# Ranking edges in a gather pass: running sums on VectorE and four TensorE products in place of sixteen

## The reference, cut to what matters

```
def _rel_graph_conv(x, W, W_loop, b, src, dst, etypes, num_nodes):
    xw = jnp.einsum('nd,rdh->rnh', x, W)
    msg = xw[etypes, src]
    agg = jax.ops.segment_sum(msg, dst, num_segments=num_nodes)
    return agg + x @ W_loop + b
h = _rel_graph_conv(features, W1, loop1, b1, src, dst, etypes, n)
h = jax.nn.relu(h)
h = _rel_graph_conv(h, W2, loop2, b2, src, dst, etypes, n)
```

## Time and profile before

| | us |
|---|---|
| median of 3 runs (12566.58 to 12575.17) | 12574.69 |
| span of the profiled execution, which is all that is known of its own time | 15198.0 |
| ranking pass g0, first gather to last, in the profile | 2704.8 |
| plain pass g1, first gather to last, in the profile | 2412.6 |

### The profile page before, as it was taken

The page is one execution under the profiler, slowest core; times in us unless marked ns, Lnnn a source line. Parts: engine busy times, 40 slices in busy tenths (PEclk is TensorE's granted clock), DMA queues, the critical chain, the costliest instruction groups (busy, mean ns, idle before and its releaser), DMA issues. The chain is left out here.

```text
span 15198.0 us, 174858 instructions
## 1 busy us (share of the span) xinstructions
PE 7352.3 (48%) x42682; PEld 5826.6 (38%) x42906; DVE 5571.9 (37%) x10022; ACT 2825.4 (19%) x7817; POOL 8278.1 (54%) x8916
## 2 busy tenths in 40 slices
PE   7444444463323324333333886777777773333332
PEld 4343333332222223333232764555555553222222
DVE  5444444431111113212111886655555654111111
ACT  4000000020000002111111004555555553000000
POOL 1555656626666664666666124444444444666665
PEclk8666666676565666556666997777777776565565
DMA  4111111141111111111111761111111111222222
GB/s 179 40 40 40 40 40 40 42 156 45 45 45 45 45 45 51 43 44 43 43 44 43 187 150 45 38 38 38 38 38 38 39 38 49 47 47 47 47 47 58
DMA packets 628740, 846.66 MB, mean 56 GB/s; under 512 B 167762, under 2 KB 464219, under 8 KB 628212
## 3 DMA queue, kind: packets, MB, share of 16 engines
q0 software_dynamic: 270448, 573.37, 14.6%
q1 hardware_dynamic: 225848, 205.13, 4.3%
q10 hardware_dynamic: 131916, 62.14, 1.6%
HBM read 598.43 MB, written 244.10 MB: 55 GB/s over the span
## 5 line engine op out<-in xcount | busy, mean ns | idle before, releaser
L1206 POOL DMA_INDIRECT GF<-TAB,IDXA x3322 | 3212.3, 967 | 2220.4 <-issue 1197.2
L1250 PE MATMUL PSUM<-GF,OH 128*128 x10560 | 2292.5, 401 | 4035.2 <-SPq L1191 2396.1
L1250 PEld LDWEIGHTS PSUM<-GF,OH 128*128 128x128 f32 x10560 | 2095.4, 302 | 4213.9 <-issue 4213.3
L1774 POOL DMA_INDIRECT GF<-HTAB,IDS x1760 | 1678.9, 954 | 1754.4 <-PE PSUM L1951 1015.8
L1123 DVE TENSOR_TENSOR OH<-PSUM,DLOA 128x1024 f32<-128x1024 f32 x660 | 804.4, 1222 | 4346.5 <-remote 1927.9
L1533 POOL DMA_INDIRECT MSG<-GF,IDS x1661 | 1610.5, 970 | 1072.7 <-ACT GF L1463 584.1
L1206 POOL DMA_INDIRECT GF<-HROW,IDXA x1661 | 1570.9, 946 | 949.3 <-issue 475.6
L1521 PE MATMUL PSUM<-ACC,SCR 128*128 x3520 | 736.5, 388 | 1198.4 <-ACT PSUM L1441 1029.4
L2031 DVE TENSOR_REDUCE SM<-PSUM 128x8 f32<-128x1024 f32 x880 | 1074.7, 1221 | 311.4 <-remote 208.0
L1521 PEld LDWEIGHTS PSUM<-ACC,SCR 128*128 128x128 f32 x3520 | 675.9, 289 | 1234.1 <-issue 1234.0
L1489 DVE CAST SCR<-PSUM 128x1024 f32<-128x1024 bf16 x220 | 269.4, 1225 | 2043.1 <-remote 1551.7
(11 more groups left out here) (388 smaller groups left out, 10841.7 us busy)
## 6 DMA issues: line engine op xcount, KB each, us to landing
GF<-MSG ACTq DMA_DIRECT2D x880, 66.0 KB, 2.2
GF<-MSG SPq DMA_DIRECT2D x880, 66.0 KB, 2.2
GF<-TAB,IDXA POOLq DMA_INDIRECT x3322
TAB<-SCR SPq DMA_DIRECT2D x100, 512.0 KB, 2.6
TAB<-OH SPq DMA_DIRECT2D x96, 512.0 KB, 2.6
GF<-HTAB,IDS POOLq DMA_INDIRECT x1760
MSG<-GF,IDS POOLq DMA_INDIRECT x1661
GF<-HROW,IDXA POOLq DMA_INDIRECT x1661
```

Of the source, the lines that this page charges most:

```text
L1206: q.indirect_dma_start(G[:, t % RING, k, 0:row], None, table, bass.IndirectOffsetOnAxis(ap=IDXA[:, at:at + 1], axis=0)).then_inc(s_got[t % ...
L1250: m = q.matmul(PSUM[:, bass.ds(places[k], w)], OH[:, r % 2, k, :], GW[:, bass.ds(rows[k], w)], start=False, stop=False, skip_group_check=True)
L1774: q.indirect_dma_start(GT[:, r, k, :], None, HTAB, bass.IndirectOffsetOnAxis(ap=IDS[:, r, k:k + 1], axis=0)).then_inc(s_got[r], 16)
```

## The change

DVE builds the one-hots with the key outermost and nine slots for each key, of which slot 0 stays zero (`KO` is 98 x 9). A `tensor_tensor_scan` over all 882 elements, with a constant `CARRY` that is 0 at slot 0 and 1 elsewhere, makes running sums of the slots into `BEFORE`, restarting at each key. Slot k of `BEFORE` then counts the tiles before tile k of the whole octet, and slot 8 counts all eight. PE needs one product with `ONESB` over these sums and one with `USTB` over the one-hots for each half: four products of 392, 392, 490 and 392 columns. The 98 extra columns are the octet's totals; DVE adds them to `SOFAR` once for each octet, and `RK` is read only once, at the start. `counted` with its eight small products, and both copies of `RK` are gone, and so are the six products of L1409. PE's moving operands, and the one-hots that DVE multiplies by, are now read with a step of nine bf16 elements (18 bytes). A new semaphore `s_one` orders the one-hots ahead of the scan; `keys` now waits for the products of the octet before the last one.

```diff
-            KO = SCR[:].rearrange("p a c -> p (a c)").bitcast(BF16)[:, 0:2 * K * NB].rearrange("p (u k b) -> p u k b", u=2, k=K)
+            wide = SCR[:].rearrange("p a c -> p (a c)").bitcast(BF16)
+            KO, BEFORE = (wide[:, i * 2 * (K + 1) * NB:(i + 1) * 2 * (K + 1) * NB].rearrange("p (u b k) -> p u b k", u=2, k=K + 1) for i in range(2))
+            CARRY = ST6[:].rearrange("p b c -> p (b c)").bitcast(BF16)[:, 0:(K + 1) * NB]
...
-            RK, WITHIN = PS[4][:, 0:NB], [PS[5 + h][:, 0:HALF * NB] for h in range(2)]
+            RK, WITHIN = PS[4][:, 0:NB], [PS[5 + h][:, 0:(HALF + h) * NB].rearrange("p (k b) -> p k b", b=NB) for h in range(2)]
...
-                        wait(q, s_rk, 2 * (t - 1) + 1)
-                        q.tensor_tensor(KO[:, r % 2], bcast(IOTP[:, 0:NB].unsqueeze(1), P, K, NB),
-                                        bcast(KEYS[:, bass.ds(t * K, K)].unsqueeze(2), P, K, NB), ALU.is_equal).then_inc(s_key, 1)
+                        wait(q, s_w, 2 * (t - 1))
+                        one = KO[:, r % 2, :, 1:K + 1]
+                        q.tensor_tensor(one, bcast(IOTP[:, 0:NB].unsqueeze(2), P, NB, K),
+                                        bcast(KEYS[:, bass.ds(t * K, K)].unsqueeze(1), P, NB, K), ALU.is_equal).then_inc(s_one, 1)
+                        q.wait_ge(s_one, t + 1)
+                        q.tensor_tensor_scan(BEFORE[:, r % 2].rearrange("p b k -> p (b k)"), CARRY,
+                                             KO[:, r % 2].rearrange("p b k -> p (b k)"), 0.0, ALU.mult, ALU.add).then_inc(s_key, 1)
...
-                        at, own_keys = PLACE[h], KO[:, r % 2, h * HALF:(h + 1) * HALF, :]
-                        q.wait_ge(s_rk, 2 * t + h + 1)
-                        q.tensor_copy(SOFAR[h], RK).then_inc(s_far, 1)
+                        at, own_keys = PLACE[h], KO[:, r % 2, :, 1 + h * HALF:1 + (h + 1) * HALF].rearrange("p b k -> p k b")
                         q.wait_ge(s_w, 2 * t + h + 1)
-                        q.wait_ge(s_far, 2 * t + h + 1)
-                        q.tensor_tensor(at, WITHIN[h].rearrange("p (k b) -> p k b", k=HALF), bcast(SOFAR[h].unsqueeze(1), P, HALF, NB),
-                                        ALU.add).then_inc(s_t, 1)
+                        if h:
+                            q.tensor_tensor(SOFAR[(r + 1) % 2], SOFAR[r % 2], WITHIN[1][:, HALF, :], ALU.add).then_inc(s_far, 1)
+                            q.wait_ge(s_far, t + 2)
+                        q.tensor_tensor(at, WITHIN[h][:, 0:HALF, :], bcast(SOFAR[r % 2].unsqueeze(1), P, HALF, NB), ALU.add).then_inc(s_t, 1)
...
-                        q.matmul(WITHIN[h], USTB[:], KO[:, r % 2, h * HALF:(h + 1) * HALF, :].rearrange("p k b -> p (k b)"), start=True, stop=False,
+                        lo = h * HALF
+                        q.matmul(WITHIN[h], ONESB[:], BEFORE[:, r % 2, :, lo:lo + HALF + h].rearrange("p b k -> p k b"), start=True, stop=False,
                                  skip_group_check=True)
-                        for k in range(HALF - 1):
-                            n = HALF - 1 - k
-                            m = q.matmul(WITHIN[h][:, (k + 1) * NB:].rearrange("p (k b) -> p k b", k=n), ONESB[:],
-                                         bcast(KO[:, r % 2, h * HALF + k, :].unsqueeze(1), P, n, NB), start=False, stop=k == HALF - 2,
-                                         skip_group_check=True)
-                        m.then_inc(s_w, 1)
-
-                    def counted(r, t, h):
...
-                        for k in range(HALF):
-                            m = q.matmul(RK, ONESB[:], KO[:, r % 2, h * HALF + k, :], start=False, stop=False, skip_group_check=True)
-                        m.then_inc(s_rk, 1)
+                        q.matmul(WITHIN[h][:, 0:HALF, :], USTB[:], KO[:, r % 2, :, lo + 1:lo + 1 + HALF].rearrange("p b k -> p k b"), start=False,
+                                 stop=True, skip_group_check=True).then_inc(s_w, 1)
```

More of the change, by code:

```diff
@@ L1302, in ranked_pass @@
                 "oh", "mm", "io", "land", "bias", "fr", "free", "kept", "open"))
-            s_kb, s_key, s_w, s_far, s_t, s_pos, s_rk = (own(tag + n) for n in ("kb", "key", "w", "far", "t", "pos", "rk"))
+            s_kb, s_one, s_key, s_w, s_far, s_t, s_pos, s_rk = (own(tag + n) for n in ("kb", "one", "key", "w", "far", "t", "pos", "rk"))
             s_got = [sem(tag + f"got{r}") for r in range(RING)]
             HALF = K // 2
-            KO = SCR[:].rearrange("p a c -> p (a c)").bitcast(BF16)[:, 0:2 * K * NB].rearrange("p (u k b) -> p u k b", u=2, k=K)
+            wide = SCR[:].rearrange("p a c -> p (a c)").bitcast(BF16)
+            KO, BEFORE = (wide[:, i * 2 * (K + 1) * NB:(i + 1) * 2 * (K + 1) * NB].rearrange("p (u b k) -> p u b k", u=2, k=K + 1) for i in range(2))
+            CARRY = ST6[:].rearrange("p b c -> p (b c)").bitcast(BF16)[:, 0:(K + 1) * NB]
             KEYS = POSA[:, 0:NTG * K]
             PLACE = [WT[:, h * HALF * NB:(h + 1) * HALF * NB].rearrange("p (k b) -> p k b", k=HALF) for h in range(2)]
-            RK, WITHIN = PS[4][:, 0:NB], [PS[5 + h][:, 0:HALF * NB] for h in range(2)]
+            RK, WITHIN = PS[4][:, 0:NB], [PS[5 + h][:, 0:(HALF + h) * NB].rearrange("p (k b) -> p k b", b=NB) for h in range(2)]
             SOFAR = [HT[:, h, 0:NB] for h in range(2)]
@@ L1388, in _ @@
                     q.tensor_copy(KEYS, KEYS.bitcast(I32)).then_inc(s_kb, 1)
-                    q.wait_ge(s_kb, 2)
+                    q.memset(CARRY, 1.0).then_inc(s_kb, 1)
+                    q.wait_ge(s_kb, 3)
+                    q.memset(CARRY.rearrange("p (b k) -> p b k", k=K + 1)[:, :, 0], 0.0).then_inc(s_kb, 1)
+                    q.memset(KO[:, :, :, 0], 0.0).then_inc(s_kb, 1)
+                    q.wait_ge(s_rk, 1)
+                    q.tensor_copy(SOFAR[0], RK).then_inc(s_far, 1)
+                    q.wait_ge(s_kb, 5)
+                    q.wait_ge(s_far, 1)
                     keys(0, 0)
@@ L1404, in within @@
                         wait(q, s_t, 2 * (t - 1) + h + 1)
-                        q.matmul(WITHIN[h], USTB[:], KO[:, r % 2, h * HALF:(h + 1) * HALF, :].rearrange("p k b -> p (k b)"), start=True, stop=False,
+                        lo = h * HALF
+                        q.matmul(WITHIN[h], ONESB[:], BEFORE[:, r % 2, :, lo:lo + HALF + h].rearrange("p b k -> p k b"), start=True, stop=False,
                                  skip_group_check=True)
-                        for k in range(HALF - 1):
-                            n = HALF - 1 - k
-                            m = q.matmul(WITHIN[h][:, (k + 1) * NB:].rearrange("p (k b) -> p k b", k=n), ONESB[:],
-                                         bcast(KO[:, r % 2, h * HALF + k, :].unsqueeze(1), P, n, NB), start=False, stop=k == HALF - 2,
-                                         skip_group_check=True)
-                        m.then_inc(s_w, 1)
-                    def counted(r, t, h):
-                        if not is_tile(t):
-                            return
-                        q.wait_ge(s_far, 2 * t + h + 1)
-                        for k in range(HALF):
-                            m = q.matmul(RK, ONESB[:], KO[:, r % 2, h * HALF + k, :], start=False, stop=False, skip_group_check=True)
-                        m.then_inc(s_rk, 1)
+                        q.matmul(WITHIN[h][:, 0:HALF, :], USTB[:], KO[:, r % 2, :, lo + 1:lo + 1 + HALF].rearrange("p b k -> p k b"), start=False,
+                                 stop=True, skip_group_check=True).then_inc(s_w, 1)
                     def body(j, r, g):
@@ L1426, in body @@
                             within(r, g, h)
-                        for h in range(2):
-                            counted(r, g, h)
                     passes(q, body)
```

## The result

The changed kernel takes 12721.87 us (12716.33 to 12726.31), the kernel before 12572.74: a ratio of 1.0117, 95% interval 1.0105 to 1.0129. It is 149 us slower, where 130 us faster was forecast.

The account below looks back on a forecast made before the run. The PE/DVE chain was taken to bound ranking pass g0 at 9.93 us a step; falling to 8.15, below the gathers' 9.51, it should save 130 us: 12575 - 130 = 12445 us, range 12330 to 12530.

Parts of the forecast that it names:

- the PE/DVE chain: Ranking pass g0: PE and DVE set the pace at 9.93 us a step, falling to 8.15.
- The bound of the gathers: Whole kernel: 8404 gathers at 1.26 us plus stages between passes make 12247 us, leaving 328 of the median for waits.
- 292: Ranking pass g0 against plain pass g1: ranking costs 292 us in the profile, the most cheaper ranking could give back.
- The effect on the gathers: POOL in g0: the scan costs the gathers nothing, since POOL's times stay 0.95 us beside L1371 with two SBUF operands.
- If the scan slows the gathers' 1.26: Sign of being wrong, in g0: the scan lengthens the 1.26 us from one gather to the next.
- The scan's price: DVE in g0: the 882-element scan takes 1.6 us, with 1.07 and 5.9 as ends.
- the prediction's foot of 0.17 us: DVE sums: fixed time of 0.17 us beside a slope of 1.02 ns an element.
- The strided reads: PE in g0: four products with an 18-byte step take 1.40 us, as fast as packed columns.
- The slower rival: PE in g0: strided products over 3.5 us make the kernel slower, 12725 us at 3 times packed; chance 0.10.
- DVE and PE hold each other no more: PE and DVE in g0: 5 us of slack, so the cycle is the longer chain, 8.15 us, not their sum.

Follow-up runs that it names:

- second profile: The kernel before, unchanged, profiled once more: 12587.14 us, profile span 12585.3 us.
- the sum alone: Kernel before plus, for each octet, one DVE sum of two fp32 SBUF operands of 1792 elements, result unused: 12792.68 us, ratio 1.0162.
- the earlier trace: First profile of the kernel before, unchanged, which the prediction read: span 15198 us.
- both operands in PSUM: Changed kernel with the scan's constant in PSUM and the sum of places written back into its PSUM bank: 12553.47 us, ratio 0.9972.
- the places in PSUM: Kernel before, no scan, with sum, product and reduce of its places run in the PSUM bank: 12620.93 us, ratio 1.0027.
- PE's program filled up: Changed kernel, scan's constant and places in PSUM, plus 144 zero-column products and 5 wait entries in PE's program: 12499.26 us, ratio 0.9940.

## Why the prediction was wrong, point by point

**What bounds the kernel.** Wrong. I took the PE/DVE chain, at 9.93 us a step, to set the pace, from a profile 2623 us longer than the median. In the second profile PE waits 249.5 us for DVE's copy rather than 506, the gathers 54.4 for the ring rather than 581.9, and the pass is 2165 us. The bound of the gathers was in the prediction itself: 8404 gathers at 1.26 us and the stages between them left 328 us of waits. That sum was right (the plain pass takes 2100 for its 2093), and it should have replaced the rows of the disturbed execution, not stood beside them. There were at most 72 us to gain in g0, and not 292. (Most of the 328 us are in the attention pass: 2476.5 us for 1760 gathers, which need 2218.)

**The effect on the gathers.** This is the step that failed in size and sign: "I cost the scan's effect on POOL at nothing". The argument was that L1371, with two SBUF operands and 0.57 us, leaves the gathers at 0.95. It does not quite. In the second profile 75 of 1566 gathers between 400 and 2440 us take over 1.0 us, all of them beside L1371, 19 us in all; they end 0.82 to 0.83 us after it, as those held by the sum alone do. What decides is which starts first: the gather of 0.95 us at 1511.96 in the earlier trace rows runs beside an L1371 that starts at 1512.28, so it was there before it, and it stands for the ones that go free. And the earlier trace rows already had POOL busy for 1616.90 us in g0 and 1595.38 in g1 with the same 1661 gathers; 103 gathers of g0 over 1.0 us lie beside an L1371 in that trace too. A hold of 0.57 us lets most gathers through, because only those that start in its first 0.4 us are held; one of 2.0 us is longer than the 1.26 between two gathers and meets one every time. "If the scan slows the gathers' 1.26" stood among the signs of being wrong, but no rival and no chance went with it. Measured: +166 us of POOL's busy time and +116 us of pass for the change; alone, the scan costs 200 us.

The Trainium skill has this rule, in "SBUF — State Buffer", section "SBUF: two separate sides": VectorE and GpSimd share one pair of ports, a VectorE operation with two SBUF inputs takes it for its whole length against a GpSimd operation that reads SBUF, and whoever comes second waits. The traces agree where the VectorE operation comes first: the gather ends 0.76 us after the scan, 208 times of 208, and the hold is gone with one of the two inputs in PSUM. The other way round they differ: a scan that starts while a gather is under way starts 0.03 us after DVE's operation before it, like all the others, and takes 1.99 to 2.03 us, so a gather does not keep the scan out for its own length.

**The scan's price.** Taken at 1.6 us, between 1.07 and 5.9; it is 2.00. (At its own rate of 1.73 ns an element the 1.6 should read 1.53; nothing hangs on it.) The Trainium skill's "DVE: opcode table, instruction layouts, handler registers and perf-mode slots", section "Datapath and trigger behaviour", says that the built-in scan runs at half throughput, and the trace agrees: with the prediction's foot of 0.17 us taken off, 882 elements in 1998 ns are 2.07 ns each and the 784 of the one-hots in 966 ns are 1.02.

**The strided reads.** Taken at the packed rate, 1.40 us for four products; from 1508.38 they start 0.72, 0.71 and 0.88 us apart, 3.0 us in all with the last one, 2.2 times as long. The Trainium skill's "SBUF — State Buffer" has in section "Door 1: The DMA port swizzle" the note on cachelines, by which each access that crosses to a new one pays; the trace agrees, with 0.71 us against 0.33. The slower rival has the right time, 12725, for a wrong reason, and that is luck: it needed 3.5 us for these products, and with both operands in PSUM the strides are all there and the pass is at the gathers' pace.

**DVE and PE hold each other no more.** Right: between sums PE now waits for landed rows, 665 us of them, as the prediction asked to see. But the shorter chain could give back only the 54.4 us for which the gathers waited, and the longer gathers cost three times that.

**Not in the prediction at all:** 28 us in a pass that the change does not touch, which go with the length of PE's program ahead of it.

## What to carry to other kernels

Hold the profiled execution's span against the median before reading a duration: where they differ by a fifth, the rows show the disturbance, and a sum over the work that can't go faster says more. Beside a pass that is bound by gathers from GpSimd, count each VectorE operation with two SBUF inputs by its length; one operand in PSUM took the cost away, for operations as long as before. It paid where PE waited for rows by hundreds of us; in the kernel before, where it did not, the same move made the pass 8 us longer. An edit that shortens or lengthens the program of one engine can move a later pass by some tens of us, so a change of 0.2% should be checked with the program's length restored. The scan's constant in PSUM, the places in PSUM and PE's program filled up turned 1.0117 into 0.9940.

## What was not expected of the hardware

A 2.0 us VectorE operation on one SBUF input cost nothing beside the gathers (ratio 0.9999), and the same length on two inputs 206 us (1.0162). A gather that starts 0.042 us after such an operation goes through, and one at 0.046 is held until it ends. Strided bf16 columns come at the same pace at 1.2 and 2.4 GHz (0.71 and 0.69 us for 392). Three entries more in PE's program, long before, cost 22 us in another pass. Why the first profile of the kernel before was disturbed stays open; no profile of the changed kernel or of the eleven experiments shows it again, though one unprofiled execution with the places in PSUM took 13718.76 us, where the other nine took 12616 to 12631.
